# Attention of both layers as one stream of 16 head groups, with everything else inside its steps

## The reference

```
x = norm(x + attn0(x))   # 16 heads of 16, 4 key heads, rope, band |i-j| <= 64, sink
x = norm(x + ffn0(x))    # down(silu(x Wg sg) * (x Wu su)) sd, int8 weights, width 1024
x = norm(x + attn1(x))   # 16 heads of 16, rope, causal over 512 tokens, biases
x = norm(x + moe(x))     # shared mlp + top 2 of 16 experts, width 176
```

## Time and profile before

| | before |
|---|---|
| median of 3 runs | 919.25 us |
| lowest, highest | 914.71, 924.97 us |
| span of the profiled execution | 921.3 us |
| PE, DVE, ACT, POOL busy, share of the span | 86%, 61%, 52%, 38% |
| chain that ended last: PE, DVE, ACT, POOL | 63%, 16%, 7%, 6% |
| idle matmuls (L1408) | 111, 34.3 us busy |

### The profile page before, as it was taken

The page is one execution under the profiler, slowest core; times in us unless marked ns, Lnnn a source line. Parts: engine busy times, 40 slices in busy tenths (PEclk is TensorE's granted clock), DMA queues, the critical chain, the costliest instruction groups (busy, mean ns, idle before and its releaser), DMA issues.

```text
span 921.3 us, 15631 instructions
## 1 busy us (share of the span) xinstructions
PE 793.3 (86%) x5464; PEld 616.0 (67%) x5473; DVE 566.3 (61%) x1439; ACT 482.0 (52%) x1019; POOL 353.5 (38%) x647
## 2 busy tenths in 40 slices
PE   6997999989788898997989988969899688899955
PEld 3775775667577665875775667758755466789845
DVE  5544578458267784663667647437684358799923
ACT  3473563865544557564534674645546433467503
POOL 7872601423546124145450241635413430255511
PEclk9897999979989999799899999989999979999978
DMA  9024000000000000000010000000170510345452
GB/s 244 2 38 80 1 1 1 2 0 3 24 1 24 24 2 2 1 3 24 1 47 1 2 2 2 2 1 1 47 283 2 142 35 13 98 138 152 133 205 92
DMA packets 26723, 43.21 MB, mean 47 GB/s; under 512 B 5972, under 2 KB 20054, under 8 KB 25784
## 3 DMA queue, kind: packets, MB, share of 16 engines
q0 software_dynamic: 6688, 23.30, 7.9%
q1 hardware_dynamic: 17248, 16.19, 6.9%
q10 hardware_dynamic: 2712, 2.73, 0.9%
HBM read 20.31 MB, written 14.60 MB: 38 GB/s over the span
## 4 chain that ended last, share of the span: by engine, by line
PE 63%; DVE 16%; ACT 7%; POOL 6%; issue 3%; DMA 2%; another core or an unknown queue 1%; ACTq 0%; SPq 0%; DVEq 0%; POOLq 0%
PE ps L1563 8%; DVE negmax L1178 7%; PE ps L1577 6%; PE ps L1550 5%; PE ps L1423 5%; PE ps L1701 4%; PE ps L1845 4%; PE ps L1484 3%; PE ps L1493 2%; PE ps L1862 2%; PE ps L1416 2%; PE ps L1680 2%; PE ps L1711 2%; PE ps L1408 2%; PE ps L1759 2%
## 5 line engine op out<-in xcount | busy, mean ns | idle before, releaser
L1178 DVE TENSOR_REDUCE negmax<-ps 128x2 fp32r<-128x512 f32 (+4 forms) x304 | 176.5, 633 | 41.4 <-PE ps L1550 38.9
L844 ACT ACTIVATE prob<-ps 128x448 f32<-128x448 f32 (+2 forms) x320 | 150.9, 525 | 52.5 <-PE ps L1563 49.9
L1550 PE MATMUL ps<-kT,qT 128*128 128x256 f32 (+4 forms) x512 | 149.0, 367 | 0.0
L1563 PE MATMUL ps<-qT,kT 128*128 128x192 f32 (+4 forms) x512 | 119.3, 318 | 10.6 <-ACT prob L844 5.3
L1563 PEld LDWEIGHTS ps<-qT,kT 128*128 128x128 f32 x512 | 79.6, 189 | 46.7 <-ACT prob L844 34.4
L658 POOL TENSOR_SCALAR_AFFINE_SELECT prob<-prob 128x512 f32<-128x512 f32 (+1 forms) x192 | 110.1, 601 | 0.0
L653 POOL TENSOR_TENSOR carry_p<-neg_half 128x1 f32<-128x1 f32 x80 | 16.4, 205 | 209.7 <-ACT prob L844 209.6
L1550 PEld LDWEIGHTS ps<-kT,qT 128*128 128x128 f32 x512 | 93.5, 196 | 2.5
L1577 PE MATMUL ps<-prob,v_aug 128*32 128x256 f32 (+4 forms) x1024 | 75.3, 400 | 13.1 <-POOL prob L658 12.6
L997 DVE TENSOR_TENSOR xT<-ps,xT 128x256 fp32r<-128x256 f32 x92 | 37.3, 422 | 72.8 <-ACT xT L728 70.6
L691 POOL DMA_INDIRECT token_y<-ys_sb,y_row x47 | 45.1, 959 | 72.6 <-DVE ys_sb L1373 72.0
(11 more groups left out here) (235 smaller groups left out, 1787.1 us busy)
## 6 DMA issues: line engine op xcount, KB each, us to landing
xs_sb<-slot_x SPq DMA_DIRECT2D x47, 129.0 KB
w_sb<-in_w POOLq DMA_DIRECT2D x4, 1408.0 KB, 11.8
...
```

What stands on the lines that cost most here:

```text
L844: act.activation(prob[:, part % PROB_BUFS, j, 0:n], ps[:, 3 + i % 3, 0:n], ACT.Exp, scale=SCALE).then_inc(exped[l].sem, 1)
L1178: dve.tensor_reduce(out=negmax[:, t, s * GH + j * mh:s * GH + (j + 1) * mh], in_=ps[:, k % 3, 0:mh * n].rearrange("p (h n) -> p h n", n=n) ...
L1550: ins = pe.matmul(dst[:, jj, :], qT[:, h // 2, t * P:(t + 1) * P], kT[:, k_block(h), k0:k0 + n], start=False, stop=True, skip_group_check= ...
L1563: ins = pe.matmul(ps[:, 3 + item % 3, col:col + n], kT[:, k_block(h), kt * P:(kt + 1) * P], qT[:, h // 2, q0:q0 + n], start=True, stop=Tru ...
```

## The change

Each layer's attention is one stream over the 16 groups of all four batches: 18 steps for 16 groups, where there were 4 x 6 for 4 x 4. The program is now: head of batch 0; stream of layer 0; FFN of all batches; stream of layer 1; experts. To fill it:

- **Turns by group.** Queries and keys are turned group by group, one step ahead, in slots 2, 4 and 6 of a step (layer 0: 12 turns of 128x128) or 5, 6, 7 and 9 (layer 1: 16). Each is copied out by DVE or ACT into a ring of four. Slot 0 of a step waits for all four copies of its group.
- **Heads** of the other batches are inside the streams (layer 0: two tiles in each of steps 0 and 1, one in steps 2 to 9; layer 1: tiles 8 to 15 in steps 2 to 9). The qkv product of tiles 0 to 7 of layer 1 is inside the FFN of batches 1 and 2.
- **Projections** of batches 0 to 2 take two tiles each in steps 7, 8, 11, 12, 15, 16; those of batch 3 stand in the FFN of batch 0 (layer 0) or after the stream (layer 1).
- **Router** and choice of experts of batches 0 to 2 are inside the stream of layer 1; the scatter of batches 2 and 3 into expert order follows it.
- **FFN** is double-buffered: the down product of batch b-1 stands after the second of eight up blocks of batch b.
- **PSUM.** To make room, raw scores and exp-scores have two banks each (0 to 3), values one (4), turned outputs one (5), all the rest 6 and 7.
- **POOL** converts the remaining weights after its part of step 0 of layer 0.
- Most idle matmuls are gone, those in the head of batch 0 are fewer.

The first place is PE at the end of attention 0 of a batch, before: values (L1577), turned outputs (L1588), then the transposes of the projection's input and its product (L1423), with what each waits for in brackets. In all three places L and a number is a line of the kernel that the rows are of.

The diff, cut to what the prediction speaks of (POOL's order, the banks, the slots, PE's orders):

```diff
-IDLE_HEAD, IDLE_STACK, IDLE_TAIL = 6, 6, 4
-IDLE_LOAD, IDLE_IN_HEAD, IDLE_IN_STACK = 8, 2, 4
...
+STEPS_OF_ATTENTION = ALL_G + 2
...
+def head_tiles(l, s):
+
+    if l == 0 and s < 2:
+        return [NT + 2 * s, NT + 2 * s + 1]
+    return [s + 6] if 2 <= s and s + 6 < TT else []
+
+
+def proj_tiles(s):
+
+    b, k = divmod(s - 7, NG)
+    return [b * NT + 2 * k, b * NT + 2 * k + 1] if 0 <= b < B - 1 and k < 2 else []
+
+
+def router_tiles(s):
+
+    if s == STEPS_OF_ATTENTION - 1:
+        return list(range(2 * NT, 3 * NT))
+    b, k = divmod(s - 9, NG)
+    return [b * NT + 2 * k, b * NT + 2 * k + 1] if 0 <= b < B - 2 and k < 2 else []
...
+            for s in range(STEPS_OF_ATTENTION):
+                g = s - 2
+                tiles, projs = head_tiles(0, s), proj_tiles(s)
+                for i in range(SLOTS[0]):
+                    if i == 2 and tiles:
+                        rest_of_head(tiles[0])
+                    if i == 5 and len(tiles) == 2:
+                        rest_of_head(tiles[1])
+                    if i == 6 and s + 2 < ALL_G:
+                        stack_k(0, s + 2)
+                    if g >= 0 and i % GH == GH - 1 and i // GH < N_PARTS[0]:
+                        keep(0, g, i // GH)
+                    if i == 6 and projs:
+                        rstd_of(0, projs[0])
+                if projs:
+                    rstd_of(0, projs[1])
+                if s == 0:
+                    rest_of_weights()
+                if s == 3:
+                    rest_of_constants()
+
+            def down_low(n):
...
+                act.wait_ge(*scored[l].ge(n + 1))
+                cols = PART_COLS[l][i // GH]
+                act.activation(prob[l][:, part % PROB_BUFS, i % GH, 0:cols], ps[:, 2 + n % 2, 0:cols], ACT.Exp,
+                               scale=SCALE).then_inc(exped[l].sem, 1)
...
+                if item >= 2:
+                    pe.wait_ge(*maxed[l].ge(item - 1))
...
+                dst = ps[:, item % 2, 0:mh * n].rearrange("p (h n) -> p h n", n=n)
...
+                    ins = pe.matmul(ps[:, 2 + item % 2, col:col + n],
...
+            def attention_slot(l, s, i):
+
+                g = s - 2
+                n_items = N_PARTS[l] * GH
+                if i == 0 and s < ALL_G:
+                    pe.wait_ge(*q_out0[l].ge(s + 1))
+                    pe.wait_ge(*q_out1[l].ge(s + 1))
+                    pe.wait_ge(*k_even[l].ge(K_TURNS[l] * (s + 1)))
+                    pe.wait_ge(*k_odd[l].ge(K_TURNS[l] * (s + 1)))
+                if i == 0 and g >= 0:
+                    pe.wait_ge(*sh_row[l][g % RING].ge(32 * (g // RING + 1)))
+                if g >= 0 and i < n_items:
+                    score_item(l, g, i)
+                if s < ALL_G and i < N_ITEMS[l]:
+                    raw_item(l, s, i)
+                if i == SHIFT_AT and 1 <= s <= ALL_G:
+                    shift_tr(l, s - 1)
+                item = g * n_items + i - PV_LAG
+                if g >= 0 and i < n_items and item >= 0 and item % GH == GH - 1:
+                    pv_part(l, item // GH)
+                if g >= 1 and i == O_AT:
+                    o_transposes(l, g - 1)
+
+            pe.wait_ge(made.sem, MADE_IDENT)
...
+            for s in range(STEPS_OF_ATTENTION):
+                tiles, projs, before = head_tiles(0, s), proj_tiles(s), proj_tiles(s - 1)
+                if s == 7:
+                    pe.wait_ge(w_lo.sem, 2)
+                headed = head_tiles(0, s - 1) if s else []
+                for i in range(SLOTS[0]):
+                    attention_slot(0, s, i)
+                    if i == 0 and tiles:
+                        head_turn(0, tiles, 7)
+                    if i == 1 and projs:
+                        if before:
+                            pe.wait_ge(*summed[0].ge(before[1] + 1))
+                        if headed:
+                            pe.wait_ge(*qkv_out.ge(headed[-1] + 1))
+                        o_turn(0, projs[0], 6)
+                    if i == 2 and s + 1 < ALL_G:
+                        if tiles:
+                            pe.wait_ge(*xh_lo[0].ge(HEAD_EVENT[0][tiles[0]] + 1))
+                        turn_q(0, s + 1, 0, 7)
+                    if i == 3 and tiles:
+                        if projs:
+                            pe.wait_ge(*aux_lo[0].ge(AUX[0]["o", projs[0]] + 1))
+                        elif before:
+                            pe.wait_ge(*summed[0].ge(before[1] + 1))
+                        if headed:
+                            pe.wait_ge(*qkv_out.ge(headed[-1] + 1))
+                        head_qkv0(tiles[0], 6)
+                    if i == 4 and s + 1 < ALL_G:
+                        pe.wait_ge(*q_out0[0].ge(s + 2))
+                        turn_q(0, s + 1, 1, 7)
+                    if i == 5 and len(tiles) == 2:
+                        pe.wait_ge(*qkv_out.ge(tiles[0] + 1))
+                        head_qkv0(tiles[1], 6)
+                    if i == 5 and projs:
+                        if tiles:
+                            pe.wait_ge(*qkv_out.ge(tiles[0] + 1))
+                        o_product(0, projs[0], 6)
+                    if i == 6 and s + 1 < ALL_G:
+                        pe.wait_ge(*q_out1[0].ge(s + 2))
+                        turn_k(0, s + 1, 0, 7)
...
+            def gate_up(n):
+
+                b, m = divmod(n, NI)
+                if m == 0:
+                    pe.wait_ge(*xf_lo.ge((b + 1) * NT // 2))
+                for w, bank, sig, free in ((wg_sb, 0, gated, silued), (wu_sb, 2, upped, fused)):
+                    if n >= 2:
+                        pe.wait_ge(*free.ge(n - 1))
...
+            for b in range(B):
+                for m in range(NI):
+                    gate_up(b * NI + m)
+                    if b == 0:
+                        if m == 1:
+                            o_transposes(0, ALL_G - 1)
+                        if m == 2:
+                            o_turn(0, last, 7)
...
+                    if b >= 1 and m == 1:
+                        downward(b - 1)
...
+                            head_turn(1, [t0, t0 + 1], 7)
...
+            for s in range(STEPS_OF_ATTENTION):
+                tiles, projs, routed = head_tiles(1, s), proj_tiles(s), router_tiles(s)
+                for i in range(SLOTS[1]):
...
+                    if i == 0 and s >= 12 and s % NG == 0:
+                        count_of(s // NG - 3, 7, 0, False)
+                    if i == 0 and tiles:
+                        head_turn(1, tiles, 7)
+                    if i == 0 and projs:
...
+                    if i == 7 and s + 1 < ALL_G:
+                        pe.wait_ge(*q_out0[1].ge(s + 2))
+                        turn_k(1, s + 1, 0, 7)
+                    if i == 9 and s + 1 < ALL_G:
+                        pe.wait_ge(*q_out1[1].ge(s + 2))
+                        turn_k(1, s + 1, 1, 6)
```

1924 lines of the change are left out of this document (1082 added, 842 removed).

## The result

| | before | changed |
|---|---|---|
| median of 20 runs | 919.32 us | 923.16 us |
| ratio | | 1.0084, 95% interval 1.0057 to 1.0111 |
| forecast | | 866 (range 832 to 920) |
| span of the profiled execution | 921.3 | 920.8 |
| mean granted clock | 0.945 | 0.907 |

A forecast was written before the change was run, and what follows sets the result against it. PE was taken as the bound, busy 793.3 of 921.3 us. Start 28, layer 0 stream 229.4, FFN 130, layer 1 stream 272.4, last projection and its turns, then experts reached 868, 53 below the profile: forecast 866, range 832 to 920.

The forecast's parts named there:

- full step of layer 0 with a head: Layer 0 stream: 8.0 us of old step, 1.3 of turns and 2.1 of waits make 11.4; a head adds 0.6.
- the border wait: Between steps, PE waits for the next group's key copies: 1.1 to 1.25 us in layer 0, 1.4 in layer 1.
- wait at the second query turn: Within a layer 0 step, PE waits until DVE has copied the first query turn: 0.85 us.
- 3.5 us of a projection: Five projections in layer 0's middle steps at 3.5 us each, from 1.9 of work and 1.17 of DVE norms: 17.5.
- 10 + 7.5 + 3 for the end of layer 0: End of layer 0's stream: step 16 takes 10 us, step 17 takes 7.5, the drain 3.
- 8 + 8.5 + 14 for the start of layer 1: Start of layer 1's stream: step 0 takes 8 us, step 1 takes 8.5, step 2 takes 14.
- 130 for the FFN: FFN of all batches: 114 us before, 21 and 3 of work added, 9 taken back by double buffering, 1 for norms.
- 11.5 + 12.5 + 9.8 + 2.5 for the end of layer 1: End of layer 1: step 16, step 17 with four router tiles, last projection with drain, and its turns, in us.
- Rival C: Clock: 5 to 10% of the streams' 500 us run at 1.2 GHz, +27 us, 893; chance 0.18.
- The 9 us: Two PSUM banks instead of three, over both streams: 4 us in layer 0 and 5 in layer 1.
- A (copies hide): At step borders ACT and DVE are always ahead, so border waits go: 34 us less, 832; chance 0.17.
- B (the chain decides, slower): In every step PE waits at all turn copies: 2.2 us more in each of 32 steps, +70, 936; chance 0.10.

The follow-up runs named there:

- Experiment 3: Changed kernel with all scores reading group 0's keys, the other groups' key copies waited for one slot later: 891.47 us, ratio 0.9719.
- Experiments 1, 2 and 6: Idle matmuls back in the changed kernel: 907.02 us; removed from the earlier kernel's batches: 929.51; at seams alone, on the changed kernel: 908.81, with turned-key/query copies earlier: 891.00.
- experiment 9: Kernel before, with two PSUM banks instead of three for raw scores and for exp-scores: 959.92 us, ratio 1.0463.
- copies_first: Changed kernel with all copies of turned queries and keys one slot earlier in the orders of DVE and ACT: 894.85 us, ratio 0.975.

## Why the prediction was wrong, point by point

**The steps themselves: right.** A full step of layer 0 with a head was forecast at 12.0 (11.4 and 0.6) and took 12.1; the border wait was forecast at 1.1 to 1.25 and is 1.2 to 1.3 where no projection stands before it. The wait at the second query turn, forecast at 0.85, is 0.71 in steps without a head and none in steps with one, whose work fills it, as the price of a head assumed. In layer 1 the 1.4 us of the border were right in size but are there at four of the borders within steps 3 to 15 only, 5.6 us where the sum held 18; that alone is more than the 8.5 us by which these steps were forecast too dear. The 3.5 us of a projection was not what its parts add up to (1.9 and 1.17 are 3.07); what it added was 3 to 4 us, and 6 in step 8, where the clock was 0.85. Experiment 3 took 12.1 and 8.4 us off these stages, in layer 1 more than the waits themselves, as the low time there went too.

**The step that failed: stages at their ends were priced like pieces of steady work.** The sum took 10 + 7.5 + 3 for the end of layer 0, 8 + 8.5 + 14 for the start of layer 1, 130 for the FFN, and 11.5 + 12.5 + 9.8 + 2.5 for the end of layer 1. The first three came out 9 to 17 us above, the last 17. Two things were missed.

- *Waits with nothing beside them.* The forecast took back all that PE waited in the FFN before and added 1 us, and it has 20.6, PE being busy for 126.9 of 147.5 (86%, where over 90% was to be seen). The three longest:

```profile
PE ps L2010 <- DVE xF L1336: 7.2, 1, 7.2
PE ps L1726 <- DVE xh L1239: 4.5, 2, 2.2
PE ps L1755 <- DVE q_st L1283: 3.7, 1, 3.7
```

In the first, the copy of batch 1's turned input stands on ACT behind a norm of batch 3, which waits for POOL, and PE's next work is batch 1. The others are the start of a chain of turn, copy and product, too. Before, such chains stood once in every batch; the change has them once a stage, and I priced them as if the double buffer hid them.

- *The clock.* Rival C, with 18%, is what happened as a mechanism: low time rose by 67 us and PE's busy time inside it by 46, so half of that, 23 us, is an estimate of the loss from the first table. C's own 893 was for the clock alone; the waits came on top. C looked for it inside the streams, and there it is only in part. Of the low time, 20 us lie in steps 3 to 15 of the two layers; 17 lie in the first three steps of each layer, 17 at the end of layer 0 and 14 in the FFN, and most of the rest from the end of layer 1 on. The five low stretches within full steps begin at or right behind border waits: at three of the four waits of 2.3 to 2.8 us behind a projection in layer 0, and at two of the five waits of 1.4 in layer 1. None begins at the seven of 1.2 to 1.3. At the seams gaps of 2.2 to 7.2 us stand at the beginning of nearly all. Two of the waits in full steps that the clock fell at:

```profile
138.52 0.50 PE L1862 MATMUL ps<-qT,kT 128*128 128x192 f32 x1 [2.75 <-DVE kT L1302]
464.71 0.47 PE L1862 MATMUL ps<-qT,kT 128*128 128x512 f32 x1 [1.41 <-DVE kT L1302]
```

Experiments 1, 2 and 6 show the cause from both sides: idle matmuls, at the seams alone or there and in the full steps, take 14 to 16 us off the change, and taking them from the kernel before adds 10. The sum costed their removal at nothing, and what they covered was the clock.

**Two banks: the price was put in the wrong steps.** The 9 us was spread over the full steps, where PE's waits for the banks are under 2 us in all. In steps with raw scores alone it is 1.1 to 1.3 us in the kernel before (experiment 9), and the change has two such steps a layer. The Trainium skill's rule on repeated gaps ("Perfetto Trace Analysis", section Optimization Strategy) holds for the kernel before with two banks, where PE waits 10.6 us more for ACT, and not for the full steps of this change, where the gap that repeats is the border's, for a key copy and not for a bank.

**The Trainium skill's rule on the clock** ("TensorE: Matmul & The Clock Gate", section A second HAM failure mode: psum-queue depth-cycling) says of a kernel that cycles through PSUM banks that short idles between groups of matmuls make the clock go back and forth. This case agrees in part: the changed kernel goes to 0.50 and back five times in its full steps, at border waits of 1.4 and of 2.3 to 2.8 us. Full steps with two banks and a border wait of 1.2 us every 12 us stay at 1.00. No run here shows that turning through banks by itself brings the clock down: the kernel before with two banks has a clock of 0.941 where it had 0.945.

**Rivals.** A (copies hide) is refuted by a wait at every border of layer 0, 1.0 us at the least; in layer 1 from step 8 on the copies do hide. B (the chain decides, slower) had the right sign and the wrong place: its 2.2 us a step more did not come.

**What stays open.** The stages' excess isn't split exactly between waits and clock, since one brings the other: copies_first took away waits only and the low time fell by 44 us. An estimate, from half of PE's busy time at 0.50, is 7 us of clock in the 9.0 at the end of layer 0, 7 in the 9.4 of the first steps of layer 1, and 5 in the 17.5 of the FFN. Experiment 1 took the low time of the first two to zero and gave back 3.7 and 5.5 net of its own work. So the clock is much of the short seams, and waits are most of the FFN. The price of two banks for raw scores in the changed kernel was not isolated. Nor were the 7.4 us of the first steps, apart from the wait of 4.8 in step 1, nor the 4.2 us of the start.
